# First layer of a two-layer image kernel: another order of the products at the end of each tile

## The reference

```
h  = w_in @ groupnorm(x)              # 64 -> 3*170 channels: gate, spatial, spectral
sp = depthwise 3x3 convolution of the spatial 170
fr = irfft2(rfft2(8x8 blocks of the spectral 170) * fft_weight)
x  = x + w_out @ (gelu(gate) * (sp + fr))    # 170 -> 64 channels
```

## Time and profile before

| | |
|---|---|
| median of 3 runs | 10444.7 us (10442.63 to 10449.47) |
| profiled execution | 10458.33 us, span 10456.5 us |
| PE busy | 9676.4 us, 93% |
| DVE busy | 8534.0 us, 82% |
| ACT busy | 5733.4 us, 55% |
| POOL busy | 1793.8 us, 17% |
| granted TensorE clock, mean | 0.957 |
| first layer of the first image | about 290 to 1500 us |
| in it, 500 to 1300 us: PE, DVE, ACT busy | 799.97, 673.72, 426.81 of 800 us; clock 1.00 |

### The profile page before, as it was taken

How to read it: one execution, slowest core, us unless ns; L and a number is a source line. 1 busy time by engine, 2 the same in 40 slices (tenths; PEclk the granted TensorE clock), 3 DMA queues, 4 the chain that set the end, 5 groups by cost and what they waited for, 6 DMA issues and landing times.

```text
span 10456.5 us, 163169 instructions
## 1 busy us (share of the span) xinstructions
PE 9676.4 (93%) x60966; PEld 7448.5 (71%) x60966; DVE 8534.0 (82%) x12871; ACT 5733.4 (55%) x9047; POOL 1793.8 (17%) x1824
## 2 busy tenths in 40 slices
PE   1999998999999998898999999899899999989998
PEld 1777765857777775675877777577687777758667
DVE  7788878978788887887878888788896888789787
ACT  0455544656755554464765555455585555446557
POOL 0000003333300001333320000223341000032334
PEclk6999999999999999998999999899999999999999
DMA  4667665465676766447567676735666666563655
GB/s 115 143 140 144 138 139 191 177 219 150 158 148 139 143 139 174 167 167 228 151 151 143 139 143 137 207 148 190 184 175 129 127 127 127 121 212 157 212 163 153
DMA packets 1332286, 1650.52 MB, mean 158 GB/s; under 512 B 843676, under 2 KB 1076524, under 8 KB 1246124
## 3 DMA queue, kind: packets, MB, share of 16 engines
q1 hardware_dynamic: 1331500, 1640.09, 61.0%
HBM read 786.71 MB, written 515.00 MB: 124 GB/s over the span
## 4 chain that ended last, share of the span: by engine, by line
PE 69%; DVE 18%; issue 5%; ACT 5%; DMA 1%; POOL 1%; SPq 1%; DVEq 0%; ACTq 0%; POOLq 0%
PE ps L819 14%; PE ps L1733 7%; PE ps L789 6%; PE ps L1746 5%; PE ps L849 4%; PE ps L780 4%; PE ps L833 4%; PE ps L1311 3%; DVE S L1515 3%; PE ps L1383 3%; PE ps L873 2%; PE ps L860 2%; DVE S L1858 2%; DVE tq L1678 2%; PE ps L795 2%
## 5 line engine op out<-in xcount | busy, mean ns | idle before, releaser
L1131 DVE SCALAR_TENSOR_TENSOR F<-U,LW,F 106x512 f32<-106x512 f32 x2048 | 1535.1, 750 | 54.4
L1733 PE MATMUL ps<-fp,Dwr 128*128 128x512 f32 x6144 | 1474.6, 389 | 0.0
L1733 PEld LDWEIGHTS ps<-fp,Dwr 128*128 128x128 f32 x6144 | 1153.3, 188 | 240.1
L1109 DVE TENSOR_TENSOR Z<-ps,LW 128x340 f32<-128x340 f32 x1024 | 522.9, 511 | 825.0 <-PE ps L789 824.0
L943 ACT ACTIVATE XF<-ps 128x340 f32<-128x340 f32 x1024 | 465.8, 455 | 1114.8 <-PE ps L780 1114.8
L819 PE MATMUL ps<-P,WP 128*128 128x512 f32 x3072 | 905.6, 417 | 31.5 <-DMA H<-P 31.5
L1311 PEld LDWEIGHTS ps<-RS,Bc 128*128 128x128 f32 x4096 | 585.5, 201 | 482.8 <-DVE RS L1300 295.1
L1746 PE MATMUL ps<-XP,Cwr 128*128 128x512 f32 x3072 | 837.2, 409 | 93.6 <-DVE XP L1870 93.6
L819 PE MATMUL ps<-H,WP 128*128 128x512 f32 x3072 | 918.3, 421 | 0.0
L1383 PE MATMUL ps<-fp,Bwr 128*128 128x512 f32 x3072 | 887.0, 429 | 21.3 <-DVE fp L1484 21.3
L1049 POOL TENSOR_SCALAR xo<-xo 64x512 f32<-64x512 f32 x4 | 6.0, 1501 | 4910.6 <-DVE xo L1165 4910.6
(11 more groups left out here) (295 smaller groups left out, 20489.9 us busy)
## 6 DMA issues: line engine op xcount, KB each, us to landing
H<-P SPq DMA_DIRECT2D x512, 585.0 KB, 7.2
raw<-x SPq DMA_DIRECT2D x240, 640.0 KB, 11.5
fx_d<-fx SPq DMA_DIRECT2D x112, 1024.0 KB, 4.0
fl_d<-fp SPq DMA_DIRECT2D x112, 1024.0 KB, 5.6
fp<-fl_d SPq DMA_DIRECT2D x112, 1024.0 KB, 5.9
fx<-fx_d SPq DMA_DIRECT2D x112, 1024.0 KB, 5.3
x1h_d<-xo SPq DMA_DIRECT2D x256, 256.0 KB, 9.0
x1v_d<-xo SPq DMA_DIRECT2D x512, 128.0 KB, 7.8
```

The source lines that it names most:

```text
L1109: e.tensor_tensor(Z[t % 2][:, 2 * c:2 * c + 2, :].rearrange("p a b -> p (a b)"), ps[6][:, 0:2 * HID], Wt, ALU.mult).then_inc(sem["z"], 1)
L1131: ins = e.scalar_tensor_tensor(o, u, wd[0:106, i:i + 1], o, ALU.mult, ALU.add)
L1733: ins = e.matmul(bank(m)[:], Dwr[:, w, c:c + 128], fq[n % 2][x][:, s2, :], start=(s2 == 0 and w == 0 and x == 0), stop=False)
```

## The change

TensorE: `conv` block 2 of half 0 moves from the start of its tile to the iteration before. At the end of an iteration the order was xs2, wout, fs2, pointwise 2, conv block 0, xs3, finv42, conv block 1, fs3; it becomes xs2, pointwise 2, conv block 0, fs2, conv blocks 1 and 2, xs3, finv42, wout, fs3. VectorE: the statistics of the next image (`gn1_dve`) move ahead of `p2`, and `x1` behind `p2`. No operation is added or removed.

```diff
             if t:
                 gate(t, 0)
                 gate(t, 1)
-                conv(t, 0, range(2, 5))
+                conv(t, 0, range(3, 5))
             finv(t, 0)
             xs(t + 1, 0)
...
             pointwise(t + 1, 1)
             xs(t + 1, 2)
-            if t == NT - 1:
-                finv42(t)
-            wout(t - 1)
-            fs(t + 1, 2)
             pointwise(t + 1, 2)
             conv(t + 1, 0, range(1))
+            fs(t + 1, 2)
+            conv(t + 1, 0, range(1, 2))
+            conv(t + 1, 0, range(2, 3))
             xs(t + 1, 3)
-            if t < NT - 1:
-                finv42(t)
-            conv(t + 1, 0, range(1, 2))
+            finv42(t)
+            wout(t - 1)
             fs(t + 1, 3)
         wout(NT - 1)
...
             if t == NT - 1:
                 fu42(t)
-            x1(t - 1)
+            if b + 1 < NB and t >= 2:
+                for i in (t - 2,) if t < 40 else (38, 39) if t == 40 else (t - 1,) if t < 50 else (49, 50) if t == 50 else (t,):
+                    gn1_dve(e, b + 1, i)
             if t == 60:
                 e.tensor_copy(raw[1][:, 9, :], ga[:, 8:9].to_broadcast([128, 258])).then_inc(sem["pad31"], 1)
                 e.wait_ge(sem["pad31"], b + 1)
             p2(t + 2)
+            x1(t - 1)
             z(t + 1, 3)
             if t < NT - 1:
                 fu42(t)
             else:
                 fl42(t)
-            if b + 1 < NB and t >= 2:
-                for i in (t - 2,) if t < 40 else (38, 39) if t == 40 else (t - 1,) if t < 50 else (49, 50) if t == 50 else (t,):
-                    gn1_dve(e, b + 1, i)
             bn(t - 1)
             depthwise(t + 1, range(4))
```

## The result

The changed kernel takes 10523.8 us (median of 4 runs, 10522.6 to 10526.7) against 10443.7 for the one before in the same comparison. The ratio is 1.0077, with a 95% interval of 1.0059 to 1.0094: slower by 80 us. The forecast was 10493, slower by 48, in a range of 10440 to 10550. So the sign and the mechanism held and the time is in the range, but the size was 32 us short.

The account below looks back on a forecast made before the run. The prediction saw TensorE alone as the bound at 18.80 us per tile, becoming a VectorE-TensorE loop of 8.12+10.89 = 19.01. 248 x 0.21 = +52.1, with special tiles +48 on 10444.7, gave 10493, range 10440 to 10550.

Parts of the forecast that it names:

- The switches: TensorE changes between half-partition and full products: four pieces fall from 3.84 to 3.53 us, saving 0.31 per tile, to 18.49.
- Rival 1: TensorE keeps the pace and the saved switches arrive whole: a gain of 77 us, 10364 with special tiles; chance 0.08.
- W to E: VectorE from the end of wout to the end of z0, x1 first: 8.12 us per tile.
- E to W: TensorE from the end of z0 through a restarted xs1 to the end of wout: 10.89 us per tile.
- The cycle: Loop through VectorE and TensorE, 8.12+10.89 = 19.01 us per tile against 18.80, 0.21 longer; bounds 18.90 to 19.14.
- z3 to z0: VectorE from start of z3 to start of z0: 6.89 us less 0.60 for the moved gn1, so 6.29.
- The sum: Tiles 1 to 62 of four images, 248 x 0.21 = +52.1 us; with -1.7, -3.8, +1.8 it is +48.
- rival 2: Saving and loop cancel: a cycle of 18.72 to 18.88 us, for instance by a cheaper restart; 10425 to 10465, chance 0.13.
- the special tiles: Tiles 40 and 50 lose stalls (-1.7 us), tile 60 its 0.96 (-3.8), the last tile of three images gains +1.8.
- What was put at nothing: Moved waits and their cover (fs2, xs3, z3, z1 and others): 0 to 0.05 us per tile, taken as 0.
- rival 3: Shifted rows H land late, pointwise 0 waits on every second tile, 124 of them: 10543 to 10617 us, chance 0.07.
- the air in the loop: Slack before TensorE waits for VectorE at xs1 in the old kernel: 0.31 us per tile, anything beyond paid in full.

Follow-up runs that it names:

- experiment 1: The changed kernel with the statistics bn also moved, one tile later and ahead of p2 on VectorE: 10365.2 us, ratio 0.9925 to the kernel before.
- experiment 7: The changed kernel with z3 moved behind the add, the first instruction of fu42, on VectorE: 10499.0 us, ratio 1.0052 to the kernel before.
- experiment 6: The changed kernel with gn1 put back between x1 and z3 on VectorE: 10638.7 us, ratio 1.0187 to the kernel before.
- experiment 2: The changed kernel's TensorE order with VectorE's old order, so p2 and gn1 stand between x1 and z0: 11039.7 us, a single run.

## Why the prediction was right, and where it was short

*The switches.* Forecast: 1.03, 0.86, 0.92 for the pair and 0.72 for the group that was behind L860. Measured: 1.02, 0.86, 0.90 and 0.72, and a TensorE tile of 18.49, forecast 18.49. The rule of the Trainium skill that the prediction quotes (TensorEngine Tiling (Array Packing), Tiling Modes, Key Properties) agrees with 0.86 for 1.01. Rival 1, which takes nothing but the saved switches (10364), was wrong for this change and fits experiment 1 (10365), in which the loop is open. One aside of the prediction the rows do not bear out, that two products of the half form run beside each other: the four of L873 take 0.86 in the stream, 0.215 each, not half of the 0.24 that each of three full ones takes. No term of the sum rests on it.

*The stretch.* W to E was put at 8.12. Measured: 817.47-809.22 = 8.25. E to W was put at 10.89 and is 827.44+0.90-817.47 = 10.87. The cycle is 19.11 to 19.16 where 19.01 was forecast. **The term that was mis-sized is x1**, 1.30 from its start to the next instruction: I had read it where p2 follows. In the stretch z3 follows, and there it is 1.42 (why, says the last section). The two ends of the rest fit: z3 to z0 816.95-810.66 = 6.29, as forecast.

*The sum.* Read from the two traces, all four images together: from L860 of tile 2 to L860 of tile 62 the changed kernel takes 18.8, 19.1, 19.1 and 19.0 longer, +76 (60 tiles of 0.34 each, less the stalls of tiles 40, 50 and 60). The start, from L888 to L860 of tile 2, is 1.5 to 1.6 shorter in each image (first image: 347.19-288.12 = 59.07 against 351.80-291.18 = 60.62), -6, because the saving is there and bn is not. The end, from L860 of tile 62 to the end of the last x1, is 1.7 longer in three images and 2.2 in the last, +7. That makes 77, against 80 between the medians (62 to 98 by the interval) and 68 between the two profiled executions.

The forecast of 48 was worked out from other parts. With 1.42 for 1.30 it would have been 248 x 0.33 - 3.7 = 78. That this is so near 80 is partly luck: it takes the first two tiles as longer, which are shorter, and the last tile as 0.6 longer in three images, where it is 1.6 to 2.1 in all four. In the first image, from the last L860 to the end of the last x1, it went from 1503.49-1492.22 = 11.27 to 1519.37-1506.53 = 12.84. Of these 1.57, gn1 ahead of x1(62) is 0.60. The rest, 0.97, is that VectorE is that much further behind TensorE here: fl42 starts 2.24 behind the start of the last L860 (1508.77 against 1506.53) and before the change 1.27. So the last but one wout now waits for it (L1146), which it did not before:

```profile
1509.43 0.98 PE L876 MATMUL ps<-FQ,WO 106*128 106x512 f32 x3 [0.94 <-DVE FQ L1146]
```

Two smaller slips of the prediction did no harm. Tile 60 costs 0.96 in three images before the change, but 1.24 in the last. And the range of rival 2, 10425 to 10465, leaves out the special tiles; with them it is 10421 to 10461.

*What was put at nothing.* fs2 behind 1.25 of cover, xs3, z1, the copies: TensorE has no other wait in the chain, and L780 is the only line of products that waits for VectorE between 500 and 1300 us, once a tile. The load of H left at 810.66, behind x1 instead of p2, and in that stretch no product waited for it. The cover was as thin as forecast, though: in three tiles of the whole run (two in the second image, one in the third) L833 waited for H, for 0.49, 0.48 and 0.63 us, and these tiles take 19.28, 19.30 and 19.45. That is rival 3 three times, not 124, and 0.6 us in all. The 7.8 us to landing were the longest of a short stretch; over the whole run before it is 7.2 in the median and up to 15.3. Rival 2 had named a restart of 0.41 for its way out; it was 0.68, as in the earlier trace rows. Here 0.41 is a piece of the chain, with the overlap cut away; in the timeline xs takes 0.57 to 0.66 in the stream. So most of the 0.27 is lost overlap with the product ahead, not a slower product.

*The evidence that carried it* was tile 40 in the earlier trace rows. A tile that by chance has one instruction more is an experiment which the kernel has made already: it gave the air in the loop (0.31) and the price of an empty pipeline.

## What to carry to other kernels

In a kernel whose chain is one engine alone, a new order of that engine moves the inputs of others; add up the way back to it through each of them before counting the gain, from the end of the product that moved to the next wait for its reader. A small piece of work that nobody waits for (here statistics of 1.19 us) belongs in the partner's waiting time, not behind the instruction that waited: the same change lost 80 us or won 77 by that alone. Take the step from one instruction to the next from a place where the same neighbour follows, and look for places where the kernel itself has a piece more (tile 40) or less (tile 1): they measure the loop before anything is changed.

## What the runs showed of the hardware

VectorE instructions usually start 0.08 us before the end that the trace gives to the one ahead: p2 or gn1 behind x1, z behind fu0, bn behind fu42. A reader of PSUM behind x1 started 0.02 to 0.04 after that end, be it z3 or the add (experiment 7), and z3 did so too with gn1 in between (experiment 6: 805.48 against 804.77+0.68) and with p2 in between (802.55 against 802.51 in the chain of experiment 2). It cost 0.11 to 0.12 a time. fu0, which reads PSUM too, does not show it behind a tap, nor z behind fu0 or the add.

What the cases with the gap have in common is not the instruction ahead, it is the last reader of PSUM before. In all of them that is the second half of x1, which reads bank 7 from partition 64 on (`ps[7][64 * p:64 * p + 64, :]` with p = 1), while z, fu and the add read from partition 0. gn1 and p2 in between read no PSUM. The cases without the gap follow a reader from partition 0. x1 itself fits: its two halves, from partition 0 and from partition 64, take 1.39 together, 0.70 from start to start for 0.69 of work, where the two of bn, with no change of partition, take 1.27, so 0.59 from start to start. A rule that says this (a reader of PSUM loses its overlap where it starts at another partition than the reader before it) fits every row read here. It was found by comparing rows; no run changed the partition alone, so it is not shown as the cause.
